# Attention and token mixing in fp32 products: squares fetched into a three-slot pair buffer, diagonal value products over visible keys, q low parts by two heads

## The chip, the cores and the metric

The kernel runs on one core of one Trainium2 chip. The metric is the device time of one execution in microseconds (us), the median of several runs. The engines are TensorE (PE), VectorE (DVE), ScalarE (ACT), GpSimd (POOL) and SyncE (SP), which here only issues DMAs.

## What is computed

The input is x of 8 x 1024 x 256. Each row is normalised to xn. The output is x plus an attention over xn plus a token-mixing network over xn:

```python
x = L0_attn_x
xn = _layernorm(x, axis=-1)
# attention: 8 query heads of 128, one shared key/value head, causal, T = 1024
q = (xn @ Wq + bq).reshape(Bsz, Tlen, 8, 128)      # then heads first, + pe
kv = xn @ Wkv + bkv
k, v = (kv[..., :128], kv[..., 128:])              # k + pe
scores = jnp.einsum('bhqd,bkd->bhqk', q, k) * scale
scores = jnp.where(causal, scores, min)
attn = jnp.einsum('bhqk,bkd->bhqd', jax.nn.softmax(scores), v)
attn_out = attn.transpose(...).reshape(Bsz, Tlen, 1024) @ Wo
# token mixing: x_prev is xn shifted by one token
xr = mu_r * xn + (1 - mu_r) * x_prev ; xk = mu_k * xn + (1 - mu_k) * x_prev
ffn_out = sigmoid(xr @ W_r.T) * (square(relu(xk @ W_k.T)) @ W_v.T)
out = x + attn_out + ffn_out
```

## The kernel before

All products are made in a two-part form: each operand is split into a high part (a ScalarE copy into the type fp32r) and a low part (the operand less its high part), and three products are added: high by high, high by low, low by high. The second index of `pt`, `v`, `wq` and so on (`pt0`, `pt1`) is the part.

**Tiling.** A batch has 64 steps. Step s belongs to query row s // 8 (128 tokens) and takes 16 of these tokens for all eight heads, 128 lines together. Its scores (L1036, `pS`) run over the width (L141): the whole key blocks of 128 before its own and (s % 8 + 1) x 16 keys of its own. Rows 0 to 3 fit in one half of a bank pair, from row 4 (step 32) on the scores are two halves.

**Way of a step.** Turn `it` of a batch does the scores of step `it`. VectorE scales and masks them into `X` and takes the row's bound (L1015, L1017). ScalarE takes the exponential (L766). VectorE takes the reciprocal of the sum (L914), GpSimd multiplies with it (L575), after it has cleared the columns of the own block behind the visible keys (L573). In the first two steps of a row (`packed`, L113) GpSimd instead writes the own block in four copies of 32 columns (L568, L569), whose high and low parts are later multiplied with a stack `vs` of value parts in one product (L1181). Then the probabilities, 128 lines by keys, must be turned. Two ways exist:

- Odd steps, and all steps of rows 0 and 1, are turned on TensorE (L1139, lag `T_LAG` = 6 turns) into `pT`; ScalarE copies the high part to `pt0` (L695), VectorE subtracts to `pt1` (L940, packed rows L945).
- Even steps from 16 on (`turned`, L108) are turned in 32 x 32 pieces by VectorE (L924, lag 3) into `Y`, stored to DRAM (`park`, L436, L442) and fetched in four transfers (`fetch`, L445, L455, lag 4) into `Z`. ScalarE copies `Z` to `pt0` (L688, lag 7), GpSimd subtracts to `pt1` (L542, lag 7), VectorE does the packed rows (L932, lag 8).

Two steps make a pair. Eight turns after its second step was scored, TensorE adds up the value products of the pair, 256 columns at a time (L1173): for each of the three passes, all key blocks k. The sum `pO` goes through ScalarE (L759) and VectorE (L994) to `ot`, and a row's output product follows (L1123).

**Fillers.** Between the steps stand products laid out by hand in `TURNS` (L33): XT (transposes of the next tokens), KV, Q (two heads each), KT, FK, FR, FV (token mixing), WO. Each Q makes `qtmp` on VectorE (L850), its high part on ScalarE (L661) and two low parts on GpSimd (L527): the first head one turn after the product, the second two turns after. FK needs `mh` (L533 on GpSimd), the scores of a new chunk of 256 keys need `kt` (L832, L837 on VectorE).

**Order.** Each engine has its own queue in program order; between engines stand semaphores. In one turn SyncE does stack, `fetch`, `park`, store, reload, in that order, and a wait holds all that is behind it. `fetch` waits for the parked square, for the low part of two squares before (L450) and, behind a packed one, for L932 (L453).

## Time and profile before

| | us |
|---|---|
| median of 3 runs | 1517.66 |
| lowest, highest | 1516.26, 1521.09 |
| profiled execution, span from first to last instruction | 1512.0 |
| mean granted clock of TensorE, share of full | 0.998 |

The profiled span is 5.7 us shorter than the median of the runs, which also hold what lies around it. The profile is read as follows. Busy time of an engine is the time in which at least one of its instructions ran. Products on TensorE overlap each other and their weight loads (PEld), so that the mean duration of one is longer than its share of the time. A group is named by line, engine, operation, output and inputs; behind the bar stand its busy time, the mean of one in ns, and the idle time of the engine in front of it with what ended it. In a timeline or chain a row has its start in us from the start of the span, its length, and how many instructions it merges.

### The profile page before, as it was taken

The page shows a single profiled execution, that of the slowest core. Times are in us where ns is not written, and L with a number is a line of the kernel's source. Part 1 is how long each engine was busy: PE and PEld are TensorE (multiplying, and loading weights), DVE is VectorE, ACT ScalarE, POOL GpSimd, SP SyncE. Part 2 cuts the span into 40 slices and gives each one's busy share as a digit, 9 for nine tenths or more (in the row PEclk, how much of TensorE's full clock was granted, in tenths as well). Part 3 has the DMA queues.
Part 4 walks back from the last instruction along what each step waited for, and adds up shares of the span by engine and source line. Part 5 has one row for each costly group of instructions (what it writes and reads, how often), then busy time and mean ns, then how long its engine had stood idle before and what let it go on. Part 6 is the DMA issues. An engine that isn't in the chain of part 4 may idle for free.

```text
span 1512.0 us, 36188 instructions
## 1 busy us (share of the span) xinstructions
PE 1484.7 (98%) x11724; PEld 1448.2 (96%) x11724; DVE 1262.6 (84%) x3424; ACT 1052.6 (70%) x2531; POOL 1153.7 (76%) x1665
## 2 busy tenths in 40 slices
PE   7999999999999999999999999999999999999998
PEld 6999999999999999999999999999999999999998
DVE  7988869888698896988879888788887988879875
ACT  5777667776677766767677676767767776777764
POOL 6787777787777787877778777778777787778774
PEclk9999999999999999999999999999999999999999
DMA  4144422444224542344423444134441344413453
GB/s 129 44 126 135 132 87 67 116 141 141 74 69 119 146 137 60 86 120 139 128 58 96 120 137 136 43 100 122 137 139 38 105 130 138 138 29 101 127 153 105
DMA packets 225801, 164.39 MB, mean 109 GB/s; under 512 B 51792, under 2 KB 220880, under 8 KB 225616
## 3 DMA queue, kind: packets, MB, share of 16 engines
q1 hardware_dynamic: 224768, 161.69, 37.1%
q8 instruction: 96, 1.57, 0.4%
q14 instruction: 89, 0.73, 0.2%
q10 hardware_dynamic: 848, 0.40, 0.1%
HBM read 81.27 MB, written 77.59 MB: 105 GB/s over the span
## 4 chain that ended last, share of the span: by engine, by line
PE 75%; DVE 10%; DMA 7%; SPq 3%; issue 3%; ACT 1%; POOL 1%; DVEq 0%; ACTq 0%; POOLq 0%
PE pS L1036 26%; PE pO L1173 21%; PE pG L1036 12%; PE pG L1123 8%; PE pT L1139 7%; DMA park_dram<-Y 5%; SPq L455 3%; DVE X L1015 2%; DVE mix L861 1%; DMA Z<-park_dram 1%; DVE Y L924 1%; DVE pt L940 1%; DVE qtmp L850 1%; PE pS L1123 1%; DVE xn L810 1%
## 5 line engine op out<-in xcount | busy, mean ns | idle before, releaser
L766 ACT ACTIVATE X<-X,bias 128x16 f32<-128x16 f32 (+56 forms) x512 | 376.0, 734 | 156.3 <-DVE bias L1015 154.8
L1036 PE MATMUL pS<-kt,qt 128*128 128x288 f32 (+41 forms) x2304 | 462.2, 329 | 4.1 <-DVE kv L837 2.5
L1173 PE MATMUL pO<-pt,v 128*128 128x256 f32 x3288 | 435.4, 283 | 2.5 <-DVE ot L994 2.4
L1173 PEld LDWEIGHTS pO<-pt,v 128*128 128x128 f32 x3288 | 399.8, 189 | 3.6 <-DVE ot L994 3.4
L575 POOL TENSOR_SCALAR X<-X,rec 128x16 f32<-128x16 f32 (+56 forms) x512 | 373.6, 730 | 26.9 <-DVE rec L914 16.2
L1015 DVE CUSTOM_DVE_ANT_0 X<-pS,mask 128x16 f32<-128x16 f32 (+56 forms) x512 | 353.7, 691 | 40.8 <-PE pS L1036 33.9
L1036 PEld LDWEIGHTS pS<-kt,qt 128*128 128x128 f32 x2304 | 365.2, 189 | 16.8 <-issue 3.7
L542 POOL TENSOR_TENSOR pt<-Z,pt 128x256 fp32r<-128x256 f32 (+5 forms) x192 | 317.7, 1655 | 78.7 <-ACT pt L688 77.8
L527 POOL TENSOR_TENSOR qt<-qtmp,qt 128x256 fp32r<-128x256 f32 x252 | 194.5, 772 | 62.8 <-ACT qt L661 55.2
L940 DVE TENSOR_TENSOR pt<-pT,pt 128x512 fp32r<-128x512 f32 (+3 forms) x440 | 207.7, 493 | 37.9 <-ACT pt L695 37.1
L759 ACT CAST ot<-pO 128x256 fp32r<-128x256 f32 x256 | 95.9, 375 | 173.4 <-PE pO L1173 94.3
L695 ACT CAST pt<-pT 128x512 fp32r<-128x512 f32 (+3 forms) x448 | 189.6, 453 | 11.8 <-PE pT L1139 11.4
L1139 PE MATMUL pT<-ident,X 128*128 128x128 f32 x1248 | 190.1, 274 | 0.8 <-DVE pt L940 0.8
L924 DVE STREAM_TRANSPOSE Y<-X 128x384 f32<-128x384 f32 (+5 forms) x192 | 172.1, 896 | 6.2 <-POOL X L575 3.8
L994 DVE TENSOR_TENSOR ot<-pO,ot 128x256 fp32r<-128x256 f32 x256 | 106.6, 416 | 83.6 <-ACT ot L759 82.1
L1123 PE MATMUL pG<-wo,ot 128*128 128x256 f32 x1344 | 169.7, 282 | 1.3 <-DVE qtmp L850 0.7
L688 ACT CAST pt<-Z 128x384 fp32r<-128x384 f32 (+5 forms) x192 | 148.1, 771 | 31.1 <-DMA Z<-park_dram 30.0
L1123 PEld LDWEIGHTS pG<-wo,ot 128*128 128x128 f32 x1344 | 160.0, 189 | 3.0 <-DVE qtmp L850 2.3
L1139 PEld LDWEIGHTS pT<-ident,X 128*128 128x128 f32 x1248 | 150.6, 141 | 9.9 <-POOL X L575 0.7
L1036 PE MATMUL pG<-xt,wq 128*128 128x256 f32 x1116 | 148.8, 283 | 1.3 <-POOL xt L515 0.8
L1036 PEld LDWEIGHTS pG<-xt,wq 128*128 128x128 f32 x1116 | 141.6, 190 | 4.5 <-DVE xtok L975 2.3
L573 POOL MEMSET X<- 128x16 f32 (+5 forms) x336 | 48.0, 143 | 105.1 <-DVE rec L914 104.5
(118 smaller groups left out, 1943.4 us busy)
## 6 DMA issues: line engine op xcount, KB each, us to landing
park_dram<-Y SPq DMA_DIRECT2D x32, 512.0 KB, 2.6
Z<-park_dram SPq DMA_DIRECT2D x128, 128.0 KB, 3.0
park_dram<-Y SPq DMA_DIRECT2D x32, 448.0 KB, 3.2
Z<-park_dram SPq DMA_DIRECT2D x128, 112.0 KB, 2.7
park_dram<-Y SPq DMA_DIRECT2D x32, 384.0 KB, 2.9
Z<-park_dram SPq DMA_DIRECT2D x128, 96.0 KB, 2.5
park_dram<-Y SPq DMA_DIRECT2D x32, 320.0 KB, 2.9
Z<-park_dram SPq DMA_DIRECT2D x128, 80.0 KB, 2.2
```

What stands on the lines that cost most here:

```text
L527: nc.gpsimd.tensor_tensor(qt[1][:, slot, :, h, :], qtmp[:, p % QTMP, i, :].rearrange("p (t q) -> p t q", q=SUB), qt[0][:, slot, :, h, :].b ...
L542: nc.gpsimd.tensor_tensor(pt_of(1, s)[:, 0:whole, :].rearrange("p k (a c) -> p a k c", a=4), Z[:, k % 2, :, 0:whole, :], pt_of(0, s)[:, 0: ...
L575: nc.gpsimd.tensor_scalar(x_row(s, 0, w), x_row(s, 0, w), rec[:, j:j + 1], 1.0, ALU.mult, ALU.mult).then_inc(normed, 1)
L695: nc.scalar.copy(pt_of(0, s)[:, k:k + nk, :], pT[u % 2][:, 0:nk * P].rearrange("p (k n) -> p k n", n=P)).then_inc(t_hi, 1)
L766: nc.scalar.activation(x_row(s, 0, w), x_row(s, 0, w), ACT.Exp, bias=bias[:, j:j + 1], scale=-1.0, accum_out=total[:, j:j + 1]).then_inc(e ...
L924: nc.vector.transpose(Y[:, k % 2, :, 0:nk, :].rearrange("p a k c -> p k a c"), x_row(s, 0, nk * P).rearrange("p (k a c) -> p k a c", a=4, ...
L940: low = nc.vector.tensor_tensor(pt_of(1, s)[:, k:k + whole, :], pT[u % 2][:, 0:whole * P].rearrange("p (k n) -> p k n", n=P), pt_of(0, s)[ ...
L1015: nc.vector.tensor_tensor_reduce(out=o, in0=scores, in1=m, scale=SCALE, scalar=HUGE, op0=ALU.add, op1=ALU.min, accum_out=bias[:, j:j + 1]) ...
L1036: last = nc.tensor.matmul(out, a[i], m[j], start=start and k == 0, stop=stop and k == n - 1)
L1123: last = nc.tensor.matmul(out[:, 0:E], ot[i][:, h, :], wo[j][:, h, :], start=(i, j, h) == (0, 0, 0), stop=i == 1 and h == H - 1)
L1139: last = nc.tensor.transpose(pT[u % 2][:, i * P:(i + 1) * P], x_row(s, (k + i) * P, (k + i + 1) * P), ident[:, :])
L1173: last = nc.tensor.matmul(pO[:, 0:2 * P], v[i][:, k, :], pt[j][:, pair % 2, k, :], start=n == 0, stop=n == 3 * nk - 1)
```

## The change

Squares that go through DRAM are no longer fetched into a buffer `Z` of their own but into the place of their low parts in `pt1`. That buffer gets three slots of a pair instead of two, and the layout of `pt` becomes: step of the pair, then 4, key block, 32. ScalarE copies from there to `pt0`, and GpSimd subtracts in place. The fetch waits until the value products of the pair three before are done. The value products read `pt` as 2 x 4 x 32 columns. For the row's own key block they take the visible keys of the pair alone, 32, 64, 96 or 128 rows of `v` and `pt`; so only even steps still clear columns behind their own, 16 of them, and VectorE clears a part of `X` once at the start. The two low parts of a Q are one GpSimd instruction, one turn after the product. `Z` is gone; the constant built there moves to `X`. The table `MODE` says for each row and pair how many of its steps go through DRAM; it holds what `turned` gave before. `EARLY` is 0, as was the early part before (its condition nk > 8 never held).

```diff
 V_LAG = 3
-H_LAG = (7, 7)
-L_LAG = (7, 8)
+F_LAG = (4, 4, 4, 4, 4, 4, 4, 4)
+H_LAG = (7, 7, 7, 7, 7, 7, 7, 7)
+L_LAG = ((7, 8), (7, 8), (7, 8), (7, 8), (7, 8), (7, 8), (7, 8), (7, 8))
+MODE = ('0000', '0000', '1111', '1111', '1111', '1111', '1111', '1111')
+SCALED = ()
+EARLY = (0, 0, 0, 0, 0, 0, 0, 0)
...
+def turns_of(s):
+
+    return int(MODE[s // H][s % H // 2])
+
+
 def turned(s):
 
-    return s >= 16 and s % 2 == 0
+    return s % 2 < turns_of(s)
...
-    return P - (s % H + 1) * SUB
+    return (s + 1) % 2 * SUB
...
-        pt = [sb(f"pt{i}", [P, 2, NT, 2 * P], R) for i in range(2)]
+        pt = [sb(f"pt{i}", [P, 2 + i, 2 * NT * P], R) for i in range(2)]
...
-        Z = sb("Z", [P, 2, 4, NT, 32])
-        steps_of = Z[:, 0, 0, 0:4, :].rearrange("p k c -> p (k c)").rearrange("p (h c) -> p h c", h=H)
+        steps_of = X[:, 9, 0:P].rearrange("p (h c) -> p h c", h=H)
...
-        def pt_of(i, s):
-
-            return pt[i][:, s // 2 % 2, :, s % 2 * P:(s % 2 + 1) * P]
+        def fetched_no(b, s):
+
+            return b * len(FETCHED) + FETCHED.index(s - s % 2)
+
+        def pair_no(b, s):
+
+            return b * (STEPS // 2) + s // 2
+
+        def pt_of(i, b, s):
+
+            nk = s // H + 1
+            return pt[i][:, pair_no(b, s) % (2 + i), 0:2 * nk * P].rearrange("p (t a k c) -> p t a k c", t=2, a=4, c=32)
...
-                k, nk = turned_no(b, s), s // H + 1
+                k, m, nk = turned_no(b, s), fetched_no(b, s), s // H + 1
+                t = s % 2
                 sp.wait_ge(turned_ready, k + 1)
-                if k >= 4:
-                    sp.wait_ge(landed[k % 4], 64 * (k // 4))
-                sp.dma_start(park_d[k % 4, :, :, 0:nk * 32],
+                if m >= 4:
+                    sp.wait_ge(landed[m % 4], 64 * (m // 4))
+                sp.dma_start(park_d[m % 4, t, :, :, 0:nk * 32],
                              Y[:, k % 2, :, 0:nk, :].rearrange("p a k c -> p a (k c)")).then_inc(parked[k % 2], 16)
 
             def fetch(b, s):
 
-                k, nk = turned_no(b, s), s // H + 1
-                sp.wait_ge(parked[k % 2], 16 * (k // 2 + 1))
-                if k >= 2:
-                    sp.wait_ge(turned_lo, k - 1)
-                    done = (k - 2) // len(TURNED), TURNED[(k - 2) % len(TURNED)]
-                    if done[1] in WITHIN:
-                        sp.wait_ge(within_lo, within_no(*done) + 1)
+                g, m, nk = pair_no(b, s), fetched_no(b, s), s // H + 1
+                tiles = turns_of(s)
+                for t in range(tiles):
+                    k = turned_no(b, s + t)
+                    sp.wait_ge(parked[k % 2], 16 * (k // 2 + 1))
+                if g >= 3:
+                    sp.wait_ge(pv_done, g - 2)
                 for q in range(4):
-                    sp.dma_start(Z[32 * q:32 * (q + 1), k % 2, :, 0:nk, :].rearrange("r a k c -> r a (k c)"),
-                                 park_d[k % 4, :, q, 0:nk * 32].rearrange("(a r) n -> r a n", a=4)
-                                 ).then_inc(landed[k % 4], 16)
+                    rows = pt[1][32 * q:32 * (q + 1), g % 3, 0:tiles * nk * P].bitcast(F)
+                    sp.dma_start(rows.rearrange("r (x n) -> r x n", n=nk * 32),
+                                 park_d[m % 4, 0:tiles, :, q, 0:nk * 32].rearrange("t (a r) n -> r (t a) n", a=4)
+                                 ).then_inc(landed[m % 4], 16)
...
+            def split_both(n, slot, p):
+                pool.wait_ge(q_hi, n * PAIRS + p + 1)
+                nc.gpsimd.tensor_tensor(qt[1][:, slot, :, 2 * p:2 * p + 2, :].rearrange("p t i q -> p i t q"),
+                                        qtmp[:, p % QTMP, :, :].rearrange("p i (t q) -> p i t q", q=SUB),
+                                        qt[0][:, slot, :, 2 * p:2 * p + 2, :].bitcast(F).rearrange("p t i q -> p i t q"),
+                                        ALU.subtract).then_inc(q_ready, 2)
+
             def split_mix(n, which):
                 pool.wait_ge(mix_hi, 2 * n + which + 1)
                 nc.gpsimd.tensor_tensor(mh[1][:, :, :], mix[:, :, :], mh[0][:, :, :].bitcast(F),
                                         ALU.subtract).then_inc(mix_split, 1)
 
             def turn(b, it):
-                for s in [s for s in TURNED if s + L_LAG[s % 2] == it]:
-                    nk = s // H + 1
-                    k = turned_no(b, s)
-                    pool.wait_ge(turned_hi, k + 1)
-                    whole = nk - packed(s)
-                    nc.gpsimd.tensor_tensor(pt_of(1, s)[:, 0:whole, :].rearrange("p k (a c) -> p a k c", a=4),
-                                            Z[:, k % 2, :, 0:whole, :],
-                                            pt_of(0, s)[:, 0:whole, :].rearrange("p k (a c) -> p a k c", a=4).bitcast(F),
-                                            ALU.subtract).then_inc(turned_lo, 1)
-                for kind, c, p in FILL[it - 2] if it > 1 else []:
-                    if absent(b, c):
-                        continue
-                    if kind == "Q":
-                        split_q(chunk_no(b, c), c % 2, p, 1)
+                for s in [s for s in TURNED if s - s % 2 + L_LAG[s // H][s % 2] == it]:
+                    whole = s // H + 1 - packed(s)
+                    pool.wait_ge(turned_hi, fetched_no(b, s) + 1)
+                    low, high = [pt_of(i, b, s)[:, s % 2, :, 0:whole, :].rearrange("p a k c -> p a (k c)") for i in (1, 0)]
+                    nc.gpsimd.tensor_tensor(low, low.bitcast(F), high.bitcast(F), ALU.subtract).then_inc(turned_lo, 1)
                 for kind, c, p in FILL[it - 1] if it else []:
                     if absent(b, c):
                         continue
                     if kind == "Q":
-                        split_q(chunk_no(b, c), c % 2, p, 0)
+                        split_both(chunk_no(b, c), c % 2, p)
...
-                for s in [s for s in TURNED if s + H_LAG[s % 2] == it]:
-                    nk = s // H + 1
-                    k = turned_no(b, s)
+                for s in [s for s in FETCHED if s + H_LAG[s // H] == it]:
+                    m = fetched_no(b, s)
                     if b or s // 2 > 1:
-                        act.wait_ge(pv_done, b * (STEPS // 2) + s // 2 - 1)
-                    act.wait_ge(landed[k % 4], 64 * (k // 4 + 1))
-                    nc.scalar.copy(pt_of(0, s)[:, 0:nk, :].rearrange("p k (a c) -> p a k c", a=4),
-                                   Z[:, k % 2, :, 0:nk, :]).then_inc(turned_hi, 1)
+                        act.wait_ge(pv_done, pair_no(b, s) - 1)
+                    act.wait_ge(landed[m % 4], 64 * (m // 4 + 1))
+                    high, raw = [pt_of(i, b, s)[:, 0:turns_of(s), :, :, :].rearrange("p t a k c -> p (t a k c)")
+                                 for i in (0, 1)]
+                    nc.scalar.copy(high, raw.bitcast(F)).then_inc(turned_hi, 1)
...
+            nc.vector.memset(X[:, 6:9, 0:E], 0.0).then_inc(x_zero, 1)
+            nc.vector.memset(X[:, 9, P:E], 0.0).then_inc(x_zero, 1)
...
+                    summed = pO[:, 0:2 * P].rearrange("p (t a c) -> p t a c", t=2, a=4)
                     work = [(k, i, j) for i, j in ((0, 0), (1, 0), (0, 1)) for k in range(plain)]
-                    early = len(work) // 2 if nk > 8 else 0
+                    early = EARLY[nk - 1] * plain
                     for n in range(early, len(work)) if part % 2 else range(early):
                         k, i, j = work[n]
                         if n == 0:
@@ -1159,10 +1181,10 @@
                                 pe.wait_ge(v_ready, b * NC + part // PER + 1)
                             if pair or not first_row:
                                 pe.wait_ge(o_lo, b * (STEPS // 2) + pair)
+                            if turned(2 * pair):
+                                pe.wait_ge(turned_hi, fetched_no(b, part) + 1)
                             for s in (2 * pair + 1, 2 * pair):
-                                if turned(s):
-                                    pe.wait_ge(turned_hi, turned_no(b, s) + 1)
-                                else:
+                                if not turned(s):
                                     pe.wait_ge(t_hi, b * T_BODY + T_FIRST[s + 1])
                         if n == 2 * plain:
                             for s in (2 * pair + 1, 2 * pair):
@@ -1170,16 +1192,18 @@
                                     pe.wait_ge(turned_lo, turned_no(b, s) + 1)
                                 else:
                                     pe.wait_ge(t_lo, b * T_BODY + T_FIRST[s + 1])
-                        last = nc.tensor.matmul(pO[:, 0:2 * P], v[i][:, k, :], pt[j][:, pair % 2, k, :],
+                        own = (part % H // 2 + 1) * 2 * SUB if k == nk - 1 else P
+                        last = nc.tensor.matmul(summed, v[i][0:own, k, :],
+                                                pt_of(j, b, part)[0:own, :, :, k, :],
...
-                            for s in (2 * pair, 2 * pair + 1):
-                                if s in WITHIN:
-                                    pe.wait_ge(within_lo, within_no(b, s) + 1)
-                            last = nc.tensor.matmul(pO[:, 0:2 * P], vs[:, part // H % TPC, :],
-                                                    pt[0][:, pair % 2, nk - 1, :], start=False, stop=True)
+                            if 2 * pair in WITHIN:
+                                pe.wait_ge(within_lo, within_no(b, 2 * pair) + 1)
+                            last = nc.tensor.matmul(summed, vs[:, part // H % TPC, :],
+                                                    pt_of(0, b, part)[:, :, :, nk - 1, :],
+                                                    start=False, stop=True)
```

The copies and subtractions of the way over TensorE (L695, L940, L945) and of the packed rows (L932) are the same operations with the new layout's patterns.

## Rows read from the trace of the kernel before

**Rows 1.** The page's line of each engine's busy time, share of the span, instructions.

```profile
PE 1484.7 (98%) x11724; PEld 1448.2 (96%) x11724; DVE 1262.6 (84%) x3424; ACT 1052.6 (70%) x2531; POOL 1153.7 (76%) x1665
```

**Rows 2.** Table of stretches: stretch, length, busy us per engine (instructions), clock, DMA.

```profile
200.00:800.00 600.00, 597.15 (x4774) 584.68 (x4773) 500.75 (x1403) 424.91 (x1045) 464.28 (x679) 1.00 0.37 105
800.00:835.00 35.00, 33.89 (x268) 32.51 (x267) 32.96 (x95) 24.09 (x63) 26.85 (x46) 1.00 0.40 106
...
860.00:1000.00 140.00, 140.00 (x1117) 137.50 (x1116) 115.44 (x318) 97.33 (x237) 107.68 (x154) 1.00 0.35 104
```

**Rows 3.** Groups of TensorE by shape: count, busy us, mean ns of one, idle before.

```profile
L1173 PE MATMUL pO<-pt,v 128*128 128x256 f32 x3288 | 435.4, 283 | 2.5 <-DVE ot L994 2.4
...
L1173 PEld LDWEIGHTS pO<-pt,v 128*128 128x128 f32 x3288 | 399.8, 189 | 3.6 <-DVE ot L994 3.4
```

**Rows 4.** Chain of work, 800 to 830 us: start, us, what.

```profile
804.20 0.69 PE pO L1173 x6
804.89 2.42 PE pS L1036 x18
```

**Rows 5.** Timeline of TensorE at turn 32 of a batch: start, us, instructions.

```profile
825.77 1.65 PE L1036 MATMUL pG<-mh,wk 128*128 128x256 f32 x12 [0.25 <-POOL mh L533]
827.67 0.98 PE L1036 MATMUL pS<-kt,qt 128*128 128x264 f32 x6 [0.24 <-DVE kv L837]
...
834.33 0.66 PE L1081 MATMUL pG<-ident,xn 128*128 128x128 f32 x4 [0.62 <-DVE xtok L975]
```

**Rows 6.** Groups of GpSimd by shape; last the fills of all shapes.

```profile
L527 POOL TENSOR_TENSOR qt<-qtmp,qt 128x256 fp32r<-128x256 f32 x252 | 194.5, 772 | 62.8 <-ACT qt L661 55.2 <-DVE rec L914 7.4
L533 POOL TENSOR_TENSOR mh<-mix,mh 128x512 fp32r<-128x512 f32 x64 | 85.0, 1328 | 0.0
...
L542 POOL TENSOR_TENSOR pt<-Z,pt 128x512 fp32r<-128x512 f32 x32 | 41.7, 1305 | 20.2 <-ACT pt L688 20.2
...
L573 POOL MEMSET X<- 128x16 f32 x64 | 7.2, 113 | 66.6 <-DVE rec L914 66.6
...
L573 POOL MEMSET X<- 128x16 f32 (+5 forms) x336 | 48.0, 143 | 105.1 <-DVE rec L914 104.5
```

**Rows 7.** Groups of ScalarE and VectorE by shape, 512 columns.

```profile
L679 ACT CAST mh<-mix 128x512 fp32r<-128x512 f32 x64 | 39.9, 624 | 24.8 <-DVE mix L861 18.4 <-PE pS L1036 6.3
...
L688 ACT CAST pt<-Z 128x512 fp32r<-128x512 f32 x32 | 19.6, 614 | 11.4 <-DMA Z<-park_dram 11.4
...
L940 DVE TENSOR_TENSOR pt<-pT,pt 128x512 fp32r<-128x512 f32 x176 | 114.8, 664 | 29.2 <-ACT pt L695 28.5
```

**Rows 8.** Waits of SyncE's queue: total us, times, longest us.

```profile
SPq L455 <- DMA park_dram<-Y: 292.0, 156, 3.5
...
SPq L453 <- DVE pt L932: 132.0, 48, 6.5
...
SPq L450 <- POOL pt L542: 29.4, 34, 2.0
```

**Rows 9.** Timelines of SyncE and TensorE around a batch's first fetch.

```profile
801.38 1.95 SPq L455 DMA_DIRECT2D Z<-park_dram  x4
...
797.10 0.96 PE L1173 MATMUL pO<-pt,v 128*128 128x256 f32 x6
```

**Rows 10.** Timeline of VectorE at the start.

```profile
0.92 0.27 DVE L865 MEMSET vs<- 32x256 f32 x1 [0.92 <-PEq L1269]
...
4.52 0.75 DVE L795 BATCH_NORM_STATS2 stats<-xtok 128x6 f32<-128x256 f32 x2 [3.33 <-DMA xtok<-x_dram]
```

**Rows 11.** Timeline of GpSimd ahead of `mh`.

```profile
822.48 0.74 POOL L527 TENSOR_TENSOR qt<-qtmp,qt 128x256 fp32r<-128x256 f32 x1
...
823.88 1.74 POOL L533 TENSOR_TENSOR mh<-mix,mh 128x512 fp32r<-128x512 f32 x1
```

**Rows 12.** Timeline of VectorE from the gate to `kt`.

```profile
822.56 0.69 DVE L966 SCALAR_TENSOR_TENSOR gate<-gate,pG 128x512 f32<-128x512 f32 x1 [0.24 <-PE pG L1036]
...
826.57 0.43 DVE L832 SCALAR_TENSOR_TENSOR kt<-kv,kt 128x256 fp32r<-128x256 f32 x1
```

46 lines of the change are left out of this document (24 added, 22 removed).

## The prediction

> **What bounds the kernel now.** I read the busy shares of the page first. TensorE is busy 98% of a span of 1512.0 us, its weight loads 96%, VectorE 84%, GpSimd 76%, ScalarE 70% [rows 1]. A high share can hide small stalls, so the table of stretches comes next. In 860 to 1000 us TensorE is busy 140.00 of 140.00 us, in 200 to 800 us it lacks 2.85 us of 600, and in 800 to 835 us it lacks 1.11 us of 35, always with the full clock of 2.4 GHz granted (1.00) [rows 2]. The losses sit in a few places and the rest is dense. How dense a stretch really is shows in the chain of work: six value products of 256 columns take 0.69 us, eighteen other products 2.42 us with score products of more columns among them [rows 4]. So one 128x256 product costs about 115 ns of TensorE's time, while the record of a single one lasts 283 ns and its weight load 189 ns [rows 3]: loads and products overlap, and the products are queued without gaps. TensorE sets the time, by its count of columns.
>
> The stalls that exist recur once in each of the eight batches, where the score products first take two halves (turn 32). In the batch shown, the FK products wait 0.25 us for GpSimd's `mh` (L533), the next scores 0.24 us for VectorE's `kv` (L837), and the transposes of the normalised tokens 0.62 us for VectorE [rows 5]. That is 1.1 us, the loss of the 35 us stretch. Eight of them are about 9 us, and nothing outside TensorE can give back much more; beside them only start and end remain.
>
> **The change, part by part.**
>
> *Order and number of work.* The new table `MODE` makes the same squares take the way through DRAM as before: even steps from row 2 on. `F_LAG`, `H_LAG` and `L_LAG` hold the old lags, and `EARLY` is zero as the old test was never true. TensorE issues the same 3288 value products and 56 stacked ones, with the same columns. By columns alone its time changes by nothing.
>
> *GpSimd, zeroing.* Before, 42 fills a batch (336, 48.0 us) clear all columns behind the visible ones. After, only even steps clear 16 columns: 4 in row 0 and 3 in each of rows 1 to 7, so 25 a batch or 200, at 0.113 us the 16-column fill, 22.6 us. That is 25 us less GpSimd time [rows 6]. The fills of L568 stay.
>
> *GpSimd, q low parts.* Of 252 single subtractions (0.772 us each) four belong to the start and stay; 248 become 124 of 512 columns. The row for a two-input subtraction of 512 columns is 1.328 us [rows 6]. The saving is 124 x (1.544 - 1.328) = 27 us, or 21 us if the runs of 16 columns cost the few per cent more (1.375 us) that a guess from the single ones allows. I take 24 us. The second head's part now comes one turn earlier, ahead of a normalisation, and waits there on ScalarE's high part, where before only the first head did. A normalisation could so start up to 0.6 us later; TensorE's transposes of it come four turns on, which is cover enough.
>
> *GpSimd, ScalarE and VectorE, layout.* The squares' high copy and low subtraction become contiguous, the direct path's writes become runs of 32. The old subtraction in runs of 32 costs 1.305 us for 512 columns and the contiguous one of L533 1.328 us [rows 6]; ScalarE's old copy in runs of 32 takes 0.614 us and a contiguous one 0.624 us; VectorE's 512-column subtraction out of PSUM takes 0.664 us [rows 7]. Runs of 32 are free in both directions, so I price all of these at zero, with 0.02 us each as the bound either way, and all of them lie beside TensorE's work.
>
> *SyncE, the fetch.* Size and number of transfers stay. The fetch no longer waits for the low part of two squares before (L450, 29.4 us, and L453, 132.0 us of queue wait); it waits until the value products of three pairs back are done. What comes last today is the parked square: 292.0 us of wait at L455 [rows 8]. For the first fetch of a batch I check the new wait: the products of that pair begin at 797.10 us and last 0.96 us, the fetch issues at 801.38 us [rows 9]. The new wait ends 3.3 us before the parked one, so nothing queued behind it on SyncE (park, store, reload) moves later. Fetches behind a packed square come up to 2.75 us earlier (132.0 / 48). ScalarE has less to wait for; TensorE does not wait there now, so this is worth zero on the path.
>
> *Start.* VectorE gets two fills more, 768 and 128 columns. The one now there takes 0.27 us for 256 columns, so about 1 us, inside the 3.33 us in which VectorE waits for the first tokens [rows 10]. Zero, and 1 us if that cover were gone.
>
> *What GpSimd's relief is worth.* 49 us less of its 1153.7 us is off the path but for the FK wait. Ahead of `mh` GpSimd works through, and its subtraction starts at 823.88 us [rows 11]. Two paired q splits and about two fills less or shorter bring it some 0.6 us earlier, so the 0.25 us go. But what is late next is VectorE: from 822.56 us it runs gate, `xtok` and masks and reaches `kt` (L832) only at 826.57 us [rows 12], and the following scores wait for that chain whenever FK ran. I credit half a microsecond for every second batch, 0.25 us x 8 = 2 us, bounds 0 and the full 9 us.
>
> *Fewer key rows on TensorE.* This is the cost that no row shows: every product in the trace is 128*128. Each batch gets 3 products with 32 rows, 24 with 64 and 24 with 96 (408 of 3288). Fewer rows stream as many columns, so there is no gain from them. A loss can come where the array changes between whole and partial rows. I count only 32 and 64 rows, the sizes that divide the array: 2 + 2 changes in row 0 and 6 in each of rows 1 to 7 (a partial product ends each of the three passes), so 46 a batch, 368 in all. Price from below: zero, as loads and products overlap now. From above: if the products before must first leave the array, 283 - 115 = 168 ns; if the weight load is exposed as well, 357 ns [rows 3]. That makes 0, 62 or 131 us. I take zero, by the 140 us without a gap in which the engine already moves between operands, banks and shapes, and because the address of the first row stays the same; the range keeps 62.
>
> The Trainium skill, page "TensorEngine Tiling (Array Packing)", section "Key Properties", says that changing the tiling mode, not merely the tile, drains the TensorE. No run here shows such a change yet; by that rule the first of the two upper prices would apply, and the rival below works it out from rows.
>
> *Moving operand in runs.* `pt` is now read as eight runs of 32 columns instead of 256 in one. No row shows TensorE reading so. Below: zero, as on the three other engines. Above: one column's time (115/256 = 0.45 ns) per run, 3.6 ns x 3288 = 12 us. I take zero, since the runs of 32 were free wherever the trace has them.
>
> **Sum.** 1512.0 + 0 (TensorE) - 2.0 (FK wait) = 1510.0 us of span. The median of the runs is 1517.66 us, 5.7 us above the profiled span, so 1515.7 us; I say 1515.5.
>
> **The rivals.**
> (B) The change of row count empties the array. For: partial and whole rows alternate inside one accumulation, 368 times, in an engine with no slack, so each nanosecond goes into the time. Against: nothing in the trace; it shows no such product. 368 x 0.168 = 62 us: 1577.5 us. This is the slower side; it decides from 13 ns a change on (368 x 13 ns = 4.8 us).
> (C) TensorE pays less than a full emptying: either a share of it (about 75 ns a change, 28 us, 1543 us) or one column per run (12 us, 1527.5 us). For: every product of this line is touched. Against: the even price on the other engines.
> (D) The stalls at turn 32 go further than I credit, since GpSimd's shorter subtractions also disturb VectorE's `mix` and `xn` less and the fetches behind packed squares land earlier. For: all three waits there hang on these engines. Against: VectorE has no idle time there. 5 to 9 us: about 1510, at best 1507.
> That the change does not do what it says is no separate case: GpSimd's relief is certain by count, and it is off the path.
>
> **How the numbers follow.** My forecast (A), 1515.5 us with its own range 1512 to 1520, has 0.43; B 0.26; C 0.16; D 0.15. A measurement here tells 0.3%, or 4.6 us, from no change. Faster is D: 0.15. Same is A: 0.43. Slower is B and C: 0.42. The range runs from 1509 us (most of D) to 1578 us (B at its first price); what lies outside is the best of D and B with exposed loads, about 0.12 together.
>
> **What would show it.** A right: value products still at 115 ns in the chain, TensorE busy all of a late 140 us stretch, GpSimd near 1105 us, L450 and L453 gone from SyncE's waits. B: value products slower in the pairs with 64 rows alone (the second pair of each row), the pairs with 96 rows at the old pace. C by runs: every value product slower, row 0 (where the runs join) excepted. D: the stalls at turn 32 gone. Wrong altogether: a wait on the fetch that reaches TensorE's L1173.

## Result and profile after

The changed kernel takes 1589.11 us (four runs, 1587.94 to 1589.47) against 1517.27 us of the kernel before: a ratio of 1.047, 95% interval 1.046 to 1.049, 71.8 us slower. The forecast was 1515.5 us; rival B, 1577.5 us, was near. The profiled execution has a span of 1587.6 us, 75.6 us more than the one of before. The part of a run outside its span is 1.7 to 3.0 us in all runs of this study. Of the 5.7 us that the prediction found between span and median, some 3 to 4 us were thus the scatter of the one execution that was profiled; the kernel before scatters from 1510 to 1521 us, the four runs of the changed one by 1.5 us.

The page of the changed kernel, its span and busy time by engine (as in [rows 1]):

```profile
span 1587.6 us, 36056 instructions
...
PE 1559.2 (98%) x11724; PEld 1479.1 (93%) x11724; DVE 1275.6 (80%) x3426; ACT 1060.6 (67%) x2531; POOL 1104.3 (70%) x1405
```

TensorE has as many instructions as before and is busy 74.5 us more. GpSimd has shed 49.4 us, and no time came of it. The table of stretches (as in [rows 2]):

```profile
200.00:800.00 600.00, 595.23 (x4517) 566.05 (x4517) 485.03 (x1306) 404.26 (x967) 421.58 (x529) 1.00 0.35 104
860.00:1000.00 140.00, 138.33 (x1028) 130.84 (x1027) 114.08 (x273) 94.95 (x207) 100.69 (x114) 1.00 0.42 126
```

The stretch of 140 us that had no gap now lacks 1.67 us, at the full clock of 2.4 GHz (1.00); 600 us lack 4.77 us instead of 2.85. So most of the 75.6 us is not idle time of TensorE but time in which it counts as busy and gets less done. The groups of value products by shape, to be read against [rows 3] (busy us, mean ns of one):

```profile
L1196 PE MATMUL pO<-pt,v 128*128 128x256 f32 x2880 | 433.7, 289 | 1.0 <-DVE ot L1015 0.9
...
L1196 PE MATMUL pO<-pt,v 64*128 64x256 f32 x192 | 69.1, 373 | 0.0
...
L1196 PE MATMUL pO<-pt,v 96*128 96x256 f32 x192 | 51.3, 284 | 0.0
...
L1196 PE MATMUL pO<-pt,v 32*128 32x256 f32 x24 | 4.9, 309 | 0.0
```

The 96-row products last 284 ns, about the 283 ns of a whole one before; the 64-row ones last 373 ns. That is the first trace of the cause. What one change of row count costs is better seen where value products meet scores. Before, behind the six products of [rows 9] (the row of TensorE there), the scores follow:

```profile
797.89 0.60 PE L1036 MATMUL pS<-kt,qt 128*128 128x320 f32 x3
```

The six products start at 797.10 us and the scores 0.79 us later. The same place in the changed kernel, a pair with 64 rows in each of its passes:

```profile
448.01 1.94 PE L1196 MATMUL pO<-pt,v 128*128 128x256 f32 x6
449.88 0.42 PE L1057 MATMUL pS<-kt,qt 128*128 128x320 f32 x1
```

Here the scores start 1.87 us after the six products, 1.08 us later than before, and in these six lie six changes: whole to 64 rows and back, three times. Two steps of the chain of work (start, us, what), one in a second and one in a third pair of the same row, say the same of a longer stretch, nine value products each:

```profile
467.65 2.02 PE pO L1196 x9
...
472.86 1.07 PE pO L1196 x9
```

The second pair (64 rows) takes 2.02 us, the third (96 rows) 1.07 us: 0.95 us for what six changes add there.

For the whole kernel I took from each trace the start of every product on TensorE and its distance to the next. Where that exceeds the median distance for its number of columns by more than 30 ns, the excess counts as a late start; the other distances give the mean spacing.

| kernel | late starts beside 32- and 64-row products, us | late starts elsewhere, us | spacing of whole value products, ns | of other 256-column products, ns |
|---|---|---|---|---|
| before | 0 | 71.3 | 116.0 | 116.3 |
| changed | 72.2 | 67.0 | 118.8 | 115.6 |
| e1_all_rows | 0 | 76.0 | 118.5 | 115.6 |
| e2_rows_before | 71.4 | 68.7 | 115.8 | 115.9 |
| e3_rows_96 | 0 | 78.2 | 118.8 | 115.7 |
| e4_adjacent | 27.1 | 65.3 | 118.6 | 115.9 |
| e5_runs | 0 | 71.7 | 118.9 | 115.7 |
| e6_rows_32 | 71.6 | 66.1 | | |
| e8_pair_64 | 27.3 | 63.2 | 118.7 | |
| e7_q_both | 0 | 83.0 | 115.9 | |
| e10_q_both_late | 0 | 75.0 | | |
| e11_q_two_early | 0 | 76.2 | | |
| e13_rows_q_undone | 0 | 71.4 | 118.5 | 115.8 |

"Elsewhere" holds real waits and also products whose records are missing, which all kernels share. Changed less before: 72.2 beside the short products, -4.3 elsewhere, +8.4 by spacing (2.8 ns x about 3000), -2.8 by the other products' spacing (some 0.6 ns closer, 4460 of them), together 73.5 of 75.6 us.

### The profile page after: what moved, and what is told of

It reads as the page before. It is cut to its first block, busy times and chain, and to the rows that moved or that the text cites. A ratio compares the mean times of both kernels' runs of the same rounds, so it can differ in the third digit from the quotient of the medians.

```text
span 1587.6 us, 36056 instructions
## 1 busy us (share of the span) xinstructions
PE 1559.2 (98%) x11724; PEld 1479.1 (93%) x11724; DVE 1275.6 (80%) x3426; ACT 1060.6 (67%) x2531; POOL 1104.3 (70%) x1405
## 4 chain that ended last, share of the span: by engine, by line
PE 91%; DVE 6%; issue 2%; DMA 0%; ACT 0%; POOL 0%; DVEq 0%; ACTq 0%
PE pS L1057 31%; PE pO L1196 27%; PE pG L1057 14%; PE pG L1144 8%; PE pT L1160 8%; PE pS L1144 1%; DVE mix L881 1%; DVE X L1036 1%; DVE xn L830 1%; DVE Y L946 1%; PE pG L1102 1%; DVE pt L961 1%; PE pS L1102 0%; PE pO L1204 0%; DVE gate L987 0%
## 5 line engine op out<-in xcount | busy, mean ns | idle before, releaser
L1196 PE MATMUL pO<-pt,v 128*128 128x256 f32 (+3 forms) x3288 | 499.1, 294 | 1.0 <-DVE ot L1015 0.9
L1057 PE MATMUL pS<-kt,qt 128*128 128x288 f32 (+41 forms) x2304 | 470.2, 332 | 10.7 <-DVE kv L857 9.3
L1196 PEld LDWEIGHTS pO<-pt,v 128*128 128x128 f32 (+3 forms) x3288 | 424.7, 188 | 41.1 <-DVE ot L1015 1.5
L594 POOL TENSOR_SCALAR X<-X,rec 128x16 f32<-128x16 f32 (+56 forms) x512 | 364.9, 713 | 49.7 <-DVE rec L936 39.0
L1057 PEld LDWEIGHTS pS<-kt,qt 128*128 128x128 f32 x2304 | 365.0, 189 | 33.0 <-DVE kt L852 10.7
L569 POOL TENSOR_TENSOR pt<-pt 128x256 fp32r<-128x256 f32 (+5 forms) x192 | 318.9, 1661 | 79.5 <-ACT pt L708 78.8
L554 POOL TENSOR_TENSOR qt<-qtmp,qt 128x512 fp32r<-128x512 f32 x124 | 161.5, 1302 | 99.4 <-ACT qt L680 89.4
L708 ACT CAST pt<-pt 128x384 fp32r<-128x384 f32 (+5 forms) x192 | 147.5, 768 | 5.2 <-DMA pt<-park_dram 5.2
L592 POOL MEMSET X<- 128x16 f32 x200 | 22.3, 111 | 144.2 <-DVE rec L936 142.1
```

What stands on the lines that cost most here:

```text
L554: nc.gpsimd.tensor_tensor(qt[1][:, slot, :, 2 * p:2 * p + 2, :].rearrange("p t i q -> p i t q"), qtmp[:, p % QTMP, :, :].rearrange("p i (t ...
L569: nc.gpsimd.tensor_tensor(low, low.bitcast(F), high.bitcast(F), ALU.subtract).then_inc(turned_lo, 1)
L594: nc.gpsimd.tensor_scalar(x_row(s, 0, w), x_row(s, 0, w), rec[:, j:j + 1], 1.0, ALU.mult, ALU.mult).then_inc(normed, 1)
L1057: last = nc.tensor.matmul(out, a[i], m[j], start=start and k == 0, stop=stop and k == n - 1)
L1196: last = nc.tensor.matmul(summed, v[i][0:own, k, :], pt_of(j, b, part)[0:own, :, :, k, :], start=n == 0, stop=n == 3 * nk - 1)
```

## The experiments

Median times of 4 to 12 runs (e6 and e8: 2 runs), and the ratio to the kernel before on the same chip:

| kernel | built on | us | ratio, 95% |
|---|---|---|---|
| e1_all_rows | changed | 1526.04 | 1.007 (1.005 to 1.009) |
| e2_rows_before | before | 1583.49 | 1.045 (1.043 to 1.047) |
| e3_rows_96 | changed | 1525.83 | 1.007 (1.005 to 1.010) |
| e4_adjacent | changed | 1543.82 | 1.019 (1.017 to 1.022) |
| e5_runs | before | 1518.12 | 1.0016 (1.0006 to 1.0027) |
| e6_rows_32 | changed | 1589.54 | 1.048 (1.046 to 1.050) |
| e8_pair_64 | changed | 1544.91 | 1.019 (1.017 to 1.021) |
| e7_q_both | before | 1525.28 | 1.0060 (1.0047 to 1.0072) |
| e10_q_both_late | before | 1517.78 | 1.0017 (1.0000 to 1.0034) |
| e11_q_two_early | before | 1519.84 | 1.0039 (1.0027 to 1.0050) |
| e9_kt_first | before | 1518.87 | 1.0025 (1.0009 to 1.0042) |
| e12_late_96b | before | 1518.27 | 1.0023 (1.0010 to 1.0035) |
| e13_rows_q_undone | changed | 1517.69 | 1.0020 (1.0006 to 1.0034) |

**Undo the rows, or do them alone.** e1 takes all 128 rows again and clears the columns as before; e2 gives the kernel before nothing but the short rows.

```diff
-                        own = (part % H // 2 + 1) * 2 * SUB if k == nk - 1 else P
+                        own = P
...
-    return (s + 1) % 2 * SUB
+    return P - (s % H + 1) * SUB
```

> The changed kernel, but every value product reads all 128 key rows again, and GpSimd clears all columns behind the visible ones as before; layout, fetch and paired q parts stay. Theory T (each change between whole and 64- or 32-row products costs TensorE about 194 ns, 71 us of starts that came late beside the 216 such products, over 368 changes): 1589 - 71 = 1518 us, plus or minus 4. Rival L (the new layout, read in runs of 32, or the fetch makes the time): stays above 1570 us.

```diff
-                        last = nc.tensor.matmul(pO[:, 0:2 * P], v[i][:, k, :], pt[j][:, pair % 2, k, :],
+                        own = (part % H // 2 + 1) * 2 * SUB if k == nk - 1 else P
+                        last = nc.tensor.matmul(pO[:, 0:2 * P], v[i][0:own, k, :], pt[j][0:own, pair % 2, k, :],
```

> The kernel before, with one edit: the value products of a row's own key block read 32, 64, 96 or 128 rows as in the change. Everything else, layout, zeroing and q parts included, is that of before. T: 1517 + 71 = 1588 us. L: 1517 us, within 0.3%.

Without the short rows the changed kernel falls to 1526.0 us; the short rows alone bring the kernel before to 1583.5 us, 68.3 us up. The rows are the cause, whatever buffers and layout surround them. Both times miss what theory T said, by 8 and 4.5 us: by the medians the rows cost 63 to 68 us, not 71. The groups of e2 by shape:

```profile
L1174 PE MATMUL pO<-pt,v 64*128 64x256 f32 x192 | 69.1, 373 | 0.0
...
L1174 PE MATMUL pO<-pt,v 96*128 96x256 f32 x192 | 50.7, 281 | 0.0
```

The same 373 and 281 ns as in the changed kernel. And e1 is still 10.9 us slower than the kernel before, which neither T nor L had foreseen: a second cost is in the change, taken up further below.

**Which rows: 96, 64 or 32.** e3 gives pairs 0 to 2 of a row 96 rows each; only the clearing behind row 96 is gone then.

```diff
-                        own = (part % H // 2 + 1) * 2 * SUB if k == nk - 1 else P
+                        own = 3 * P // 4 if k == nk - 1 and part % H < 6 else P
...
-    return (s + 1) % 2 * SUB
+    return (3 * P // 4 if s % H < 6 else P) - (s % H + 1) * SUB
```

> The changed kernel, reading 96 rows where it reads 32 or 64 (and where it reads 96), with the columns cleared up to there. In the trace after, a 96-row product starts its successor after 120 ns like a whole one. T: as fast as with all rows, about 1518 us, no late starts beside the 96-row products. Rival N (fewer rows cost by themselves, in proportion to how many are left out): between, 1530 us or more, since 408 products still leave out rows.

The time is that of e1 (1525.8 and 1526.0 us), with 408 products of 96 rows at 288 ns, against 285 ns for its whole ones:

```profile
L1197 PE MATMUL pO<-pt,v 128*128 128x256 f32 x2880 | 417.9, 285 | 1.1 <-DVE ot L1016 0.9
L1197 PE MATMUL pO<-pt,v 96*128 96x256 f32 x408 | 108.4, 288 | 0.1
```

Going from 128 to 96 rows and back costs nothing that a median shows. e6 puts 32 rows in the place of 64.

```diff
+                        own = 32 if own == 64 else own
```

> The changed kernel with 32 rows where it reads 64 (it leaves out keys 32 to 63 of the own block in the second pair of a row). T, the price is of the change and not of the number of rows: 1589 us, within 5 us. Rival: a price that grows as rows get fewer, 1610 us or more.

1589.5 us, the time of the changed kernel. The group of 32-row products:

```profile
L1197 PE MATMUL pO<-pt,v 32*128 32x256 f32 x216 | 73.8, 365 | 0.0
```

365 ns for 32 rows, 373 for 64, and 71.6 us of late starts against 72.2: the two sizes cost the same, and it isn't rows that are paid for.

**Per change or per product.** If each short product were slow by itself, their number would count; if the change costs, only the borders do. e4 puts the three products of the own block side by side at the end of a pair: as many short products, 144 changes instead of 368. The wait for the low parts moves to the first product that reads them (`first_low`).

```diff
+                    work.sort(key=lambda x: x[0] == nk - 1)
+                    first_low = [j for k, i, j in work].index(1)
...
-                        if n == 2 * plain:
+                        if n == first_low:
```

> The changed kernel, where the three products of a pair over its own key block stand together at the end of the pair instead of one at the end of each pass. The same 216 products of 32 and 64 rows, but 18 changes of row count a batch instead of 46, 144 in all. T: 1518 + 144 x 0.194 = 1546 us. Rival N (a price for each such product, 71/216 = 0.33 us, whatever stands beside it): 1589 us as in the change.

1543.8 us; three quarters of what the rows cost are gone (17.8 of 63.1 us above e1 are left) with two fifths of the changes (144 / 368 = 0.39). The timeline of TensorE in e4, a second pair:

```profile
625.87 1.16 PE L1198 MATMUL pO<-pt,v 128*128 128x256 f32 x6
626.96 0.71 PE L1057 MATMUL pS<-kt,qt 128*128 128x320 f32 x3
```

The six products, three of them with 64 rows, and the scores behind them start 1.09 us apart: 0.30 us more than the 0.79 us of before, for two changes instead of six. e8 raises the number of short products instead: the whole second pair of each row with 64 rows, 864 products, and again 144 changes.

```diff
+                        own = 64 if part % H // 2 == 1 else own
```

> The changed kernel, but in the second pair of each row all value products read 64 rows, not only those of the own block (it leaves out half of each earlier key block there). 864 products of 64 rows instead of 192, but 18 changes of row count a batch instead of 46. T, a price per change: 144 changes, like the run with adjacent products, 1544 us. Rival N, a price per product with 64 rows: 1700 us or more.

1544.9 us, with 864 short products of 286 ns each:

```profile
L1197 PE MATMUL pO<-pt,v 64*128 64x256 f32 x864 | 119.4, 286 | 0.1
```

That is the mean of a whole one. A product of 64 rows among its like costs what a whole one costs; the change is what is paid. Late starts per change: 72.2 / 368 = 0.196 us in the changed kernel, 71.4 / 368 = 0.194 in e2, 27.1 / 144 = 0.188 in e4, 27.3 / 144 = 0.190 in e8. The medians give less, (1589.1 - 1526.0) / 368 = 0.171, 68.3 / 368 = 0.186 in e2 and 17.8 / 144 = 0.124 in e4. Probably the stops take in waits that would come anyway: e1 has 9 to 11 us more of late starts elsewhere than the kernels with changes (76.0 against 67.0 and 65.3).

**The moving operand in runs.** e5 lets the value products of the kernel before read `pt` as eight runs of 32 columns. Its output columns are then in another order.

```diff
-                        last = nc.tensor.matmul(pO[:, 0:2 * P], v[i][:, k, :], pt[j][:, pair % 2, k, :],
+                        last = nc.tensor.matmul(pO[:, 0:2 * P].rearrange("p (a t c) -> p a t c", a=4, t=2), v[i][:, k, :],
+                                                pt[j][:, pair % 2, k, :].rearrange("p (t a c) -> p a t c", t=2, a=4),
```

> The kernel before, but TensorE reads the 256 columns of a value product as eight runs of 32 in an order that cannot be joined, as in the change; pt itself and all other engines are as before. The columns of the attention output come out in another order than the reference's, which no instruction's time depends on. In the trace after, whole value products start 118.8 ns apart on average and 116.0 ns before; this run asks if the runs make that. Theory R: 118.5 ns or more, 3288 x 2.6 ns = 8 to 9 us above before, 1524 us. Rival: 116 ns and the time of before, the 11 us that the all-rows run keeps come from other engines' waits.

The spacing of theory R came, its time did not. Value products start 118.9 ns apart instead of 116.0, and in the table 118.5 to 118.9 in every kernel that reads in runs, 115.8 to 116.0 in every one that doesn't. That would be 3288 x 2.9 ns = 9.5 us. But e5 is 1.9 us above the kernel before on its chip by the medians, 2.4 us by the ratio. The profiled executions differ by 7.1 us; e5's stands 2.7 us above the median of its runs and the one of before below that of its own. What gives the rest of the 9.5 us back is not shown; the other 256-column products, which start some 0.6 ns closer in e5 (about 3 us), are a part of it.

**The q low parts.** e7 brings the merged and earlier subtraction into the kernel before: the old single ones of both turns are gone, `split_both` takes the place of the first.

```diff
-                        split_q(chunk_no(b, c), c % 2, p, 1)
...
-                        split_q(chunk_no(b, c), c % 2, p, 0)
+                        split_both(chunk_no(b, c), c % 2, p)
```

> The kernel before, with only the two low parts of a Q made by one GpSimd instruction, one turn after the product. My forecast's step: 2 us faster, the FK stall of turn 32 gone and nothing else. Rival V: GpSimd's mh subtraction now runs beside VectorE's xtok (L970), which then takes longer than its 1.18 us as in the trace after (1.66 us), so that kt and the next scores come later: no gain, or up to 5 us slower.

It costs 9 us, most of what e1 had left over, and more than the forecast (2 us faster) or rival V (up to 5 us slower) allowed. V's wait is not there either: the scores wait 0.7 us for `kv` in e7, 2.5 us before. TensorE's waits in e7 (total us, times, longest):

```profile
PE pG L1038 <- POOL mh L540: 5.3, 8, 0.8
...
PE pS L1125 <- ACT ot L761: 2.7, 3, 1.1
```

The wait for `mh` was 2.8 us before (longest 0.9), the one for `ot` at this place nothing. At its longest, the one for `ot` comes about thus. ScalarE in e7 waits for a fetched square, and only then comes to `ot`; TensorE waits behind:

```profile
999.25 0.51 ACT L690 CAST pt<-Z 128x384 fp32r<-128x384 f32 x1 [2.59 <-DMA Z<-park_dram]
...
1000.56 0.37 ACT L761 CAST ot<-pO 128x256 fp32r<-128x256 f32 x1
```

```profile
1001.08 1.17 PE L1125 MATMUL pS<-wo,ot 128*128 128x256 f32 x8 [1.09 <-ACT ot L761]
```

A wait of 2.59 us on ScalarE ends in 1.09 us on TensorE. To part merging from place, e10 keeps the merged subtraction in the later of the two turns, and e11 keeps two single ones but both in the earlier.

```diff
-                        split_q(chunk_no(b, c), c % 2, p, 1)
+                        split_both(chunk_no(b, c), c % 2, p)
...
-                        split_q(chunk_no(b, c), c % 2, p, 0)
```

> The kernel before, with the two low parts of a Q in one GpSimd instruction as in the change, but two turns after the product (where the second head's part stood) instead of one. The same instruction with one turn early cost 9 us. Theory E (the early place costs: the subtraction now stands ahead of a normalisation and waits there for ScalarE's high part, so the squares of that row go late through DRAM): back at before, within 0.3%, or 1 to 3 us faster. Rival M (the merged 512-column instruction costs by its length or pattern): 1522 us or more.

```diff
-                        split_q(chunk_no(b, c), c % 2, p, 1)
...
                         split_q(chunk_no(b, c), c % 2, p, 0)
+                        split_q(chunk_no(b, c), c % 2, p, 1)
```

> The kernel before, with the two low parts of a Q as two instructions, but both one turn after the product. E: the cost of the merged early one is met or exceeded, 1525 us or more, since GpSimd then has about 0.2 us more to do in that place. M: the time of before.

By the ratios, merged but late costs 2.5 us and two early 5.9 us (4.6 by the medians), so the place looks the larger part, though the intervals overlap, and the two about add up to the 9 us of e7. E's first figure held within 0.3%, its second (1525 us or more for e11) did not, and neither did M's for either. TensorE's waits for `mh` and `ot`, in e10, e11 and before:

```profile
PE pG L1041 <- POOL mh L540: 6.0, 8, 0.8
PE pS L1128 <- ACT ot L764: 2.2, 3, 1.2
```

```profile
PE pG L1032 <- POOL mh L533: 1.4, 4, 0.5
PE pS L1119 <- ACT ot L755: 0.3, 1, 0.3
```

```profile
PE pG L1036 <- POOL mh L533: 2.8, 7, 0.9
```

Both waits are long in e10, where the long instruction stands late, and short in e11, where two short ones stand early. So they go with the long instruction, 1.3 us in one piece, and not with the place. ScalarE's wait for fetched squares isn't longer in all either: 29.2 us in e7 and 26.9 us in e11, 30.0 us before. What the earlier place costs is spread. Of e11's 4.9 us more of late starts (one execution against one) 2.9 us stand in front of value products and 1.5 us each in front of scores and of transposes of `X`; in front of FK there are 1.5 us less. No single wait explains them, and by which path the earlier place costs time stays open.

**Turn 32.** e9 exchanges KT and FV in the fillers ahead of it, so that `kt` is ready for the scores; e12 gives GpSimd the relief that costs no change of row count, 96 rows with less clearing and the merged late q parts, in the kernel before.

```diff
-     (14, "FV", 0, 0),
-     (15, "KT", 1, 0)),
+     (14, "KT", 1, 0),
+     (15, "FV", 0, 0)),
```

> The kernel before, with KT and FV of the second chunk of keys exchanged (KT in turn 30, FV in turn 31), so that VectorE's kt no longer stands behind gate and xtok when the scores of turn 32 need it. If VectorE's chain is what holds those scores, the 0.24 us in front of them go and up to 0.6 us of the XT wait with them, eight times: 1512 us. Rival: the gate work moves behind turn 32's work and holds that instead, no change or slower.

```diff
-    return P - (s % H + 1) * SUB
+    return (3 * P // 4 if s % H < 6 else P) - (s % H + 1) * SUB
...
-                        split_q(chunk_no(b, c), c % 2, p, 1)
+                        split_both(chunk_no(b, c), c % 2, p)
...
-                        split_q(chunk_no(b, c), c % 2, p, 0)
...
+                        own = 3 * P // 4 if k == nk - 1 and part % H < 6 else P
```

> The kernel before with what seems free of cost of the change: own key blocks read with 96 rows in the first three pairs of a row and GpSimd clearing columns only up to there, and the merged q parts at the late place. About 40 us less GpSimd work than before, no change of array mode, no early wait. If GpSimd's relief is worth anything: 1512 us. Rival: nothing, 1516 us, since GpSimd bounds only a few starts at turn 32.

Both missed: 1518.9 and 1518.3 us, 0.2% slower than the kernel before by intervals that leave out no change. In e9 the scores' wait for `kv` is gone and the one for `xtok` has grown from 4.1 to 10.7 us; VectorE does the same work in another order. In e12 GpSimd is busy 1122.1 us, 31.6 us less than before, and that buys nothing: the wait for `mh` has grown to 5.5 us, as with the long instruction in e7 and e10.

**All but buffers, layout and runs undone.** e13 is e1 with the old q parts as well.

```diff
+                        split_q(chunk_no(b, c), c % 2, p, 1)
...
-                        split_both(chunk_no(b, c), c % 2, p)
+                        split_q(chunk_no(b, c), c % 2, p, 0)
```

> The changed kernel with both suspects undone: all 128 key rows (with the old zeroing) and the q parts head by head at the old places. What is left of the change is the layout read in runs of 32, the three-slot buffer and the fetch into it. Theory: only the runs' 2.4 us are left, 1517.7 us. Rival: fetch or layout cost something of their own, 1521 us or more.

1517.7 us, as expected, a ratio of 1.002. The group of its value products:

```profile
L1202 PE MATMUL pO<-pt,v 128*128 128x256 f32 x3288 | 443.4, 285 | 1.1 <-DVE ot L1021 0.9
```

So the three-slot buffer, the new wait of the fetch, the layout on three engines and the fills at the start together cost no more than the runs do, some 3 us. By the medians, each above the kernel before on its own chip or above one another, the change is thus 63 us of rows (changed less e1), 8 us of q parts (e1 less e13) and 3 us for all the rest.

## Why the prediction was right or wrong

**What bounds the kernel** held in the main: 72 us of late starts on TensorE come back as 63 to 68 us of time, and 49 us less of GpSimd as none. That every nanosecond of TensorE shows in full did not hold: of the 9.5 us of wider spacing in e5 some 2 us arrive.

**Fewer key rows** is the step that failed. The count of 368 was right, and so was the place (64 rows only, 96 at the old pace). The price was chosen as zero because TensorE moved between operands, banks and shapes for 140 us without a gap. But no row of those was a product with fewer rows, so the argument did not bear on the case. In place of 0 the term measured 63 us (changed less e1) to 68 us (e2 less before), 0.17 to 0.20 us for each of the 368 changes, nearly all of the 71.8 us. The Trainium skill's rule stood in the text and spoke against the choice: "TensorEngine Tiling (Array Packing)", "Key Properties", by which a change of tiling mode drains the engine. The runs agree with it (e4 and e8: the borders cost, not the products) for 32 and 64 rows; with 96 rows they show no such cost.

**Rival B** was the mechanism with a price of 0.168 us a change, from 283 - 115 ns. It measured 0.19 to 0.20 by starts, 0.171 to 0.186 by medians. One 64-row product between whole ones shows where that goes (median of 80 such): the distance to it is 91 ns too long, the one behind it 192 ns, the next 105 ns, 388 ns for two changes. In the pair of the fence above, where whole and short ones alternate, starts are 314 to 319 ns apart from the second on, and each weight load begins only together with its product (448.306 and 448.307 us), where between whole products it starts some 115 ns ahead (before: 797.304 and 797.419 us). So part of the load seems to be exposed, which these records suggest and no run isolates; the price lies between the two of the prediction (168 and 357 ns), near the lower. With the cost of the earlier q parts this carried the time 11 us past the range's upper end, which allowed B only its lowest price and nothing beside it.

**Moving operand in runs**: taken at zero, bounded by 12 us, measured 2 to 3 us of time and 2.5 to 2.9 ns a product. The sign named for it is there: in row 0, where the runs join, e13's value products start 115.8 ns apart as before (40 distances); in e5, where they don't join even there, 118.6 ns. Copies of runs that were free on three other engines did not speak for TensorE.

**GpSimd** by its own terms was right. Its groups after:

```profile
L554 POOL TENSOR_TENSOR qt<-qtmp,qt 128x512 fp32r<-128x512 f32 x124 | 161.5, 1302 | 99.4 <-ACT qt L680 89.4 <-DVE rec L936 9.9
...
L592 POOL MEMSET X<- 128x16 f32 x200 | 22.3, 111 | 144.2 <-DVE rec L936 142.1
```

Fills 48.0 to 22.3 us (forecast 22.6); a paired q part 1302 ns, so 124 x (1.544 - 1.302) = 30 us saved (27 forecast, 24 taken); in all 1104.3 us (1105).

**q parts one turn earlier** was called free, covered by four turns, and merging them was priced only as GpSimd's saving. That failed: the earlier place alone costs 4.6 to 5.9 us (e11), merging alone 2.5 us (e10), both 9 us (e7). The step looked at one consumer, the transposes of the delayed normalisation, and at nothing else behind the instruction on GpSimd. For merging that is `mh` above all; for the place it stays open, as said above.

**The credit at turn 32** of 2 us did not come. The timeline of TensorE there:

```profile
478.86 1.58 PE L1057 MATMUL pG<-mh,wk 128*128 128x256 f32 x12
481.59 0.97 PE L1057 MATMUL pS<-kt,qt 128*128 128x264 f32 x6 [1.16 <-DVE kv L857]
```

FK no longer waits ([rows 5]), and what is late next was named rightly: the scores wait 1.16 us for VectorE. But GpSimd's relief is not what ended FK's wait. e2 has none of it (GpSimd busy 1147.6 us) and its FK products of this place don't wait for `mh` either, while e1 and e7, with TensorE at its old pace and the merged q parts, wait 4.0 and 5.3 us, more than the 2.8 us of before. The wait goes because the short rows slow TensorE. TensorE's waits in all, changed and before:

```profile
PE pS L1057 <- DVE kv L857: 9.3, 8, 1.2
PE pG L1102 <- DVE xtok L996: 3.4, 8, 0.5
```

```profile
PE pS L1036 <- DVE kv L837: 2.5, 7, 1.3
```

9.3 us for `kv` instead of 2.5, and 10.7 us in e2; in e1, without the short rows, it is 1.4 us. VectorE in the changed kernel ahead of it, and the same instruction before ([rows 12] is the same stretch):

```profile
476.79 1.66 DVE L991 SCALAR_TENSOR_TENSOR xtok<-gate,xtok 128x512 f32<-128x512 f32 x1
...
480.49 0.42 DVE L852 SCALAR_TENSOR_TENSOR kt<-kv,kt 128x256 fp32r<-128x256 f32 x1
```

```profile
823.28 1.18 DVE L970 SCALAR_TENSOR_TENSOR xtok<-gate,xtok 128x512 f32<-128x512 f32 x1
```

`xtok` takes 1.66 us instead of 1.18. In the changed kernel GpSimd's subtraction for `mh` (476.61 us) runs beside it; before, it started only at 823.88 us [rows 11], 0.6 us after `xtok` did. The other traces agree that the overlap goes with the slower `xtok`: in the changed kernel the 8 of 32 that GpSimd's subtractions cover throughout take 1.65 to 1.68 us, the 24 that none touches 0.69 to 1.13 us (one 1.50); in e2 the 8 covered ones take 1.85 to 1.86 us, the 16 untouched ones 0.69 to 0.80 us (one 1.18). No run took one of the two away alone. By e12 and e13, the latter with this wait at 3.0 us, the whole place is worth no time that can be measured.

**The fetch** went as said on the path. SyncE's queue (total us, times, longest), as in [rows 8]:

```profile
SPq L475 <- DMA park_dram<-Y: 326.4, 169, 3.8
SPq L461 <- DVE Y L946: 276.8, 130, 6.2
...
SPq L472 <- PE pO L1196: 58.7, 50, 2.0
SPq L472 <- PE pO L1204: 22.2, 10, 2.7
```

L450 and L453 are gone. The new wait, at zero in the step, is 80.9 us long in all. The check made for the first fetch of a batch did not hold for every other, but SyncE has room: e13, which keeps it at 58.7 us, loses nothing by it that can be told from the cost of the runs. ScalarE's wait for landed squares is 5.2 us in the changed kernel and 30.0 us in the one before, but that is again TensorE's slower pace: 3.0 us in e2, with the old fetch, and 24.8 us in e13, with the new one. **Layout and start** at zero were right, again by e13; with 512 columns ScalarE's copy of a square took 0.608 us (0.614 before), GpSimd's subtraction 1.292 (1.305) and VectorE's 0.663 (0.664).

**Rival C** had its two prices in the wrong sizes: a change costs 0.12 to 0.20 us, not 0.075, and the runs 2 to 3 us, not 12. **Rival D**'s gain did not come; e12 and e9 speak against it.

## What to carry to other kernels

On an engine that sets the time, an operation that no row of the trace shows must not be priced at zero because all the others are free; price it between its bounds and let the range hold the dearest rival with its upper price. Cutting the rows of a product saved no time here (286 ns for 64 rows among their like, 285 ns for 128); where it must be done, stay at 96 rows or more, or put the short products side by side so that few borders are left. A subtraction moved one turn earlier on a queue is priced by all that stands behind its wait, not by its own consumer alone. And a wait that is gone in a slower kernel is no gain of the change: look for it in a kernel where the engine that waited keeps its pace.

## What the hardware showed

- A border between products of 128 rows and of 32 or 64 costs TensorE 0.19 to 0.20 us by late starts (products of 256 columns; 368 borders in three kernels, 144 in two others) and 0.12 to 0.19 us by medians, the same for 32 as for 64 rows; with 96 rows 0 to 3 ns.
- A product with 64 rows among its like has the mean of a whole one, 286 ns.
- A moving operand in eight runs of 32 columns spaces 256-column products 2.5 to 2.9 ns wider, 2.2 to 2.5%, of which a fraction arrived in the median time (e5: 2 of 9.5 us).
- Two GpSimd subtractions of 256 columns (0.77 us each) made into one of 512 (1.31 to 1.34 us) left GpSimd 24 us less busy and cost the kernel 2.5 us (e10).
- VectorE's three-input operation of 512 columns took 1.65 to 1.86 us with GpSimd subtractions beside it throughout, mostly 0.69 to 1.13 us without (no run isolates it).
- The single execution that a profile shows can stand 4 us from the median (e3: 1529.9 and 1525.8 us): sums should be made against the span but compared by medians.
